# Mixing the spectral matrices inside the layer norm's stage, on three engines

## The chip, the cores and the metric

One core of a Trainium2 chip. The metric is device microseconds (us) of one execution; the kernel before takes 3382.94 us (median of 3 runs, 3381.09 to 3384.28). Abbreviations as in the profile: PE is TensorE's matrix multiplications, PEld its loads of stationary data, DVE is VectorE, ACT is ScalarE, POOL is GpSimd, SP is the engine that issues the DMAs.

## The reference, cut to what matters

The kernel computes a network of four layers on an image of 2 x 128 channels x 64 x 64. The change touches the second half of layer 2, a spectral filter over tokens that comes behind a layer norm:

```python
t = t + _L2_ffn_ref(_ln_t(t), sigma, phi, M_u, M_phi_plus, M_phi_minus, log_weights, gumbel)

y_soft  = softmax(log_weights + gumbel)                  # 4 weights
weights = one_hot(argmax(y_soft)) - y_soft + y_soft
# for each of the 4 branches i, on the first T // 2**i tokens:
out_i = stu(x_i, sigma ** 0.25, phi, M_u[i], M_phi_plus[i], M_phi_minus[i])
return sum(stacked * weights)
```

`M_phi_plus` and `M_phi_minus` are 4 x 16 matrices of 128 x 128, `M_u` is 4 x 3 of them. Since each branch is linear in its matrices, the kernel first sums the four branches' matrices with the four weights, and transforms once. The layer norm before it (`_ln_t`: over the 128 channels of each token) does not depend on these matrices, nor they on it.

## The kernel before, in words

The image lies in SBUF as X, 128 channels by 8192 tokens, in 16 chunks of 512 columns. The program is a sequence of stages. Each is one `Block` with a stream of instructions for each engine, semaphores between them, and a barrier of all engines at its end (`Stage.block`, L66 to L70); the instruction streams are written out by hand, and an engine runs its stream in order.

`spectral_bank` (L1722) runs, one after another: `mixing_weights` (L1242), `layer_norm_channels` with tag "sp" (L708), `spectral_inputs` (the transform, L1366), `spectral_slots`, `spectral_outputs`. The first two matter here.

`mixing_weights`. SP loads four small vectors, then `raw_u`, then four pieces of the large matrices (2 MB each: eight filters of plus or of minus, four branches) into two buffers, `raw[0]` and `raw[1]`; pieces 2 and 3 wait until DVE has finished with the buffer. DVE computes the four weights in a chain of operations on 128x4 (L1311 to L1332), with one Exp on ACT (L1293), and POOL raises sigma to the power 0.25 (L1281). Then, for each of four pieces, DVE sums the branches in four operations on 128x1024 (a tensor_scalar at L1339, three scalar_tensor_tensor at L1341) into `mixed[i]`, and multiplies it by sigma's power (L1354). It sums the direct matrices `Mu` the same way (128x384). POOL forms plus minus minus and plus plus minus into `both` (L1287), ACT rounds `both` to the high part `Mh` (L1298), and DVE at the end subtracts to get the low part `Ml` (L1362). PE has nothing to do in this stage.

`layer_norm_channels`. For each chunk c PE multiplies by the centring matrix (L734) into one of three PSUM banks `psC`; ACT squares it (L775) and copies it centred to its place (L776); PE sums the squares over channels (L742) into a row of `psV[b]`, one image half b for eight chunks. When eight chunks are summed, ACT takes the square root (L780, issued behind chunk 9 for b = 0 and behind chunk 15 for b = 1); DVE takes the reciprocal (L788) and splits it into a high and a low row (L790, L792); PE spreads it over the partitions (L753) into one of three banks `psR`; DVE multiplies the centred chunk by it (L805). In PE's order the spread of chunk c - 10 comes behind the variance of chunk c, and the last ten spreads come at the end; a spread waits until DVE has taken the chunk three before it. SP and POOL have nothing to do in this stage.

Of the kernel before, what the change touches and what calls it, by code (L numbers as in the profile page):

```python
# [15 lines left out]
ALU = mybir.AluOpType  # L16
ACT = mybir.ActivationFunctionType
AX = mybir.AxisListType
# [6 lines left out]
NCH = L // CH  # L25
# [16 lines left out]
NF = 16  # L42
# [665 lines left out]
def layer_norm_channels(nc, T, src, dst, tag, affine=None):  # L708
# [6 lines left out]
    with ExitStack() as ctx:  # L715
# [9 lines left out]
        S = Stage(nc, ctx, ["c_in_psum", "squared", "centred", "v_summed", "sd_done", "rstd_done", "rows_high",  # L725
                            "rows_done", "r_in_psum", "scaled", "z_done"])
        with S.block() as block:
            @block.tensor
# [40 lines left out]
            @block.scalar  # L769
            def _(e):  # L770
                for c in range(NC2):
                    e.wait_ge(S["c_in_psum"], c + 1)
                    if c >= 3:
                        e.wait_ge(S["v_summed"], c - 2)
                    e.activation(sq[c % 3][:, :], psC[c % 3][:, :], ACT.Square).then_inc(S["squared"], 1)  # L775
                    e.activation(centred(c), psC[c % 3][:, :], ACT.Copy).then_inc(S["centred"], 1)  # L776
                    if c == NCH + 1 or c == NC2 - 1:
                        b = c // NCH if c == NC2 - 1 else 0
                        e.wait_ge(S["v_summed"], (b + 1) * NCH)
                        e.activation(sd[b][:, :], psV[b][0:NT, :], ACT.Sqrt, bias=T["eps"][0:NT, 0:1]).then_inc(S["sd_done"], 1)  # L780

            @block.vector
            def _(e):
                for b in range(B):
                    e.memset(rows[b][64:128, :].bitcast(F32), 0.0)
                for b in range(B):
# [7 lines left out]
                    for c in range(b * NCH, (b + 1) * NCH):  # L794
# [9 lines left out]
                        else:  # L804
                            e.tensor_tensor(dst(c), psR[c % 3][:, :], centred(c), ALU.mult).then_inc(S["scaled"], 1)  # L805

# [431 lines left out]
UPAD = 4  # L1238
# [3 lines left out]
def mixing_weights(nc, T, G):  # L1242

    with ExitStack() as ctx:
        sb, _ = allocator(nc, ctx, "_mix")
        z, g, e1, y, oh, wt = (sb("mx_" + n, [128, 4]) for n in ("z", "g", "e", "y", "oh", "w"))  # L1250
        m1, s1, r1, free = (sb("mx_" + n, [128, 1]) for n in ("m", "s", "r", "free"))
        sig, quarter = sb("mx_sig", [128, NF]), sb("mx_quarter", [128, NF])
        raw = [sb(f"mx_raw{i}", [128, 4, NF // 2 * 128]) for i in range(2)]
        raw_u = sb("mx_rawu", [128, 4, 3 * 128])
        mixed = [sb(f"mx_mixed{i}", [128, NF // 2, 128]) for i in range(4)]
        both = [sb(f"mx_both{i}", [128, NF // 2, 128]) for i in range(4)]
        S = Stage(nc, ctx, ["small_loaded", ("mat_loaded", 4), "mu_loaded", "chain", "sig_done", "acc_step",
                            "both_done", "high_done", "split_done"])
        with S.block() as block:
            @block.sync  # L1260
            def _(e):
                row = lambda n: T[n][0, :].partition_broadcast(128)
                loads = [(z, row("log_weights")), (g, row("gumbel")), (sig, row("sigma")),
                         (quarter, T["c_quarter"])]
                for dst, src in loads:
                    e.dma_start(dst[:, :], src).then_inc(S["small_loaded"], 16)
                e.dma_start(raw_u[:, :, :], T["m_u"].rearrange("d i t e -> d i (t e)")).then_inc(S["mu_loaded"], 16)
                for part in range(2):
                    for n, name in enumerate(("m_plus", "m_minus")):
                        i = 2 * part + n  # L1270
                        if i >= 2:
                            e.wait_ge(S["acc_step"], 5 * (i - 1))
                        k0 = part * NF // 2
                        e.dma_start(raw[i % 2][:, :, :], T[name][:, :, k0:k0 + NF // 2, :].rearrange("d i k e -> d i (k e)"))\
                            .then_inc(S["mat_loaded"][i], 16)
                e.wait_ge(S["mat_loaded"][3], 16)

            @block.gpsimd
            def _(e):
                e.wait_ge(S["small_loaded"], 64)  # L1280
                e.tensor_tensor(sig[:, :], sig[:, :], quarter[:, :], ALU.pow).then_inc(S["sig_done"], 1)  # L1281
                e.memset(G["U"][:, 0, 0:UPAD], 0.0)
                e.memset(G["U"][:, 1, 0:UPAD], 0.0)
                for part in range(2):
                    e.wait_ge(S["acc_step"], 10 * (part + 1))
                    for n, op in enumerate((ALU.subtract, ALU.add)):
                        e.tensor_tensor(both[2 * part + n][:, :, :], mixed[2 * part][:, :, :], mixed[2 * part + 1][:, :, :], op)\  # L1287
                            .then_inc(S["both_done"], 1)

            @block.scalar  # L1290
            def _(e):
                e.wait_ge(S["chain"], 3)
                e.activation(e1[:, :], z[:, :], ACT.Exp).then_inc(S["chain"], 1)  # L1293
                for i in range(4):
                    e.wait_ge(S["both_done"], i + 1)
                    part, n = divmod(i, 2)
                    k0 = part * NF // 2
                    e.activation(G["Mh"][n][:, k0:k0 + NF // 2, :], both[i][:, :, :], ACT.Copy).then_inc(S["high_done"], 1)  # L1298

            @block.vector  # L1300
            def _(e):
                count = [0]

                def link(op):

                    count[0] += 1
                    op.then_inc(S["chain"], 1)
                    e.wait_ge(S["chain"], count[0])

                e.wait_ge(S["small_loaded"], 64)  # L1310
                link(e.tensor_tensor(z[:, :], z[:, :], g[:, :], ALU.add))  # L1311
                link(e.tensor_reduce(m1[:, :], z[:, :], AX.X, ALU.max))
                link(e.tensor_scalar(z[:, :], z[:, :], m1[:, 0:1], None, ALU.subtract))
                count[0] += 1
                e.wait_ge(S["chain"], 4)
                link(e.tensor_reduce(s1[:, :], e1[:, :], AX.X, ALU.add))
                link(e.reciprocal(r1[:, :], s1[:, :]))
                link(e.tensor_scalar(y[:, :], e1[:, :], r1[:, 0:1], None, ALU.mult))
                link(e.tensor_reduce(m1[:, :], y[:, :], AX.X, ALU.max))

                link(e.tensor_scalar(oh[:, :], y[:, :], m1[:, 0:1], None, ALU.is_ge))
                for i in range(1, 4):
                    link(e.tensor_reduce(s1[:, :], oh[:, 0:i], AX.X, ALU.add))
                    link(e.tensor_scalar(free[:, :], s1[:, :], -1.0, 1.0, ALU.mult, ALU.add))
                    link(e.tensor_tensor(oh[:, i:i + 1], oh[:, i:i + 1], free[:, :], ALU.mult))
                link(e.tensor_tensor(wt[:, :], oh[:, :], y[:, :], ALU.subtract))
                link(e.tensor_tensor(wt[:, :], wt[:, :], y[:, :], ALU.add))

                for c in range(NCH):
                    n = sum(c < NCH >> i for i in range(4))  # L1330
                    op = e.tensor_reduce(G["keep"][:, c:c + 1], oh[:, 0:n], AX.X, ALU.add)
                link(op)  # L1332
                steps = [0]

                def mix(dst, src):

                    for i in range(4):
                        if i == 0:
                            op = e.tensor_scalar(dst, src(i), wt[:, 0:1], None, ALU.mult)  # L1339
                        else:  # L1340
                            op = e.scalar_tensor_tensor(dst, src(i), wt[:, i:i + 1], dst, ALU.mult, ALU.add)  # L1341
                        steps[0] += 1
                        op.then_inc(S["acc_step"], 1)
                        e.wait_ge(S["acc_step"], steps[0])

                e.wait_ge(S["sig_done"], 1)
                for part in range(2):
                    k0 = part * NF // 2
                    for i in (2 * part, 2 * part + 1):
                        e.wait_ge(S["mat_loaded"][i], 16)  # L1350
                        dst = mixed[i][:, :, :]
                        mix(dst.rearrange("d k e -> d (k e)"), lambda x, i=i: raw[i % 2][:, x, :])
                        steps[0] += 1
# [1092 lines left out]
```

## Time and profile before

| | us |
|---|---|
| median of 3 runs | 3382.94 (3381.09 to 3384.28) |
| profiled execution, its own time | 3384.74 |
| its span | 3383.0 |
| PE busy, share of the span | 3071.9, 91% |
| DVE busy | 1908.1, 56% |
| ACT busy | 1419.0, 42% |
| POOL busy | 1056.3, 31% |

Times in the profile are counted from the start of the span. "Busy" is time in which an engine executes, summed; a stage may leave the busiest engine with nothing to do however high its share of the whole. The granted clock (PEclk) is the TensorE clock, 1.00 for 2.4 GHz and 0.50 for 1.2 GHz. An arrow "<-" in brackets names what ended an engine's idle time before the row.

### The profile page before, as it was taken

The page shows a single profiled execution, that of the slowest core. Times are in us where ns is not written, and L with a number is a line of the kernel's source. Part 1 is how long each engine was busy: PE and PEld are TensorE (multiplying, and loading weights), DVE is VectorE, ACT ScalarE, POOL GpSimd, SP SyncE. Part 2 cuts the span into 40 slices and gives each one's busy share as a digit, 9 for nine tenths or more (in the row PEclk, how much of TensorE's full clock was granted, in tenths as well). Part 3 has the DMA queues.
Part 4 walks back from the last instruction along what each step waited for, and adds up shares of the span by engine and source line. Part 5 has one row for each costly group of instructions (what it writes and reads, how often), then busy time and mean ns, then how long its engine had stood idle before and what let it go on. Part 6 is the DMA issues. An engine that isn't in the chain of part 4 may idle for free. (4 is left out here: it accounts for less than half of the span.)

```text
span 3383.0 us, 60840 instructions
## 1 busy us (share of the span) xinstructions
PE 3071.9 (91%) x23047; PEld 2397.8 (71%) x23047; DVE 1908.1 (56%) x3737; ACT 1419.0 (42%) x3058; POOL 1056.3 (31%) x1104
## 2 busy tenths in 40 slices
PE   5999997688873989999999999999889998999699
PEld 4777775233432568888888888888868887888555
DVE  5556585577525345555555555555336776776365
ACT  2555553111232234444444444444125666667200
POOL 3445450377521044444444444444000000000000
PEclk9999998799986999999999999999779999999799
DMA  7988850000002355454545455554200000000000
GB/s 173 186 181 181 179 152 20 13 1 1 1 3 109 140 74 76 72 79 69 79 72 82 72 76 76 73 79 69 62 6 1 1 1 1 1 1 1 8 22 28
DMA packets 407112, 213.33 MB, mean 63 GB/s; under 512 B 313972, under 2 KB 386316, under 8 KB 405036
## 3 DMA queue, kind: packets, MB, share of 16 engines
q1 hardware_dynamic: 388960, 199.27, 30.9%
q10 hardware_dynamic: 17868, 10.19, 1.4%
q8 instruction: 187, 3.06, 0.4%
q14 instruction: 97, 0.79, 0.1%
HBM read 177.82 MB, written 52.89 MB: 68 GB/s over the span
## 5 line engine op out<-in xcount | busy, mean ns | idle before, releaser
L1670 DVE TENSOR_TENSOR sl_vl_slot<-sl_psV_slot,sl_vh_slot 128x512 fp32r<-128x512 f32 x1024 | 636.1, 684 | 563.8 <-ACT sl_vh_slot L1649 563.8
L1649 ACT ACTIVATE sl_vh_slot<-sl_psV_slot 128x512 fp32r<-128x512 f32 x1024 | 529.3, 604 | 584.4 <-PE sl_psV_slot L1617 584.4
L85 PE MATMUL sl_psY_slot<-sl_vl_slot,sp_Mh_sp 128*128 128x256 f32 x2048 | 603.9, 295 | 0.0
L86 PE MATMUL sl_psY_slot<-sl_vh_slot,sp_Ml_sp 128*128 128x256 f32 x2048 | 577.8, 282 | 0.0
L87 PE MATMUL sl_psY_slot<-sl_vh_slot,sp_Mh_sp 128*128 128x256 f32 x2048 | 576.8, 282 | 0.0
L85 PEld LDWEIGHTS sl_psY_slot<-sl_vl_slot,sp_Mh_sp 128*128 128x128 f32 x2048 | 389.1, 190 | 91.0 <-issue 90.6
L86 PEld LDWEIGHTS sl_psY_slot<-sl_vh_slot,sp_Ml_sp 128*128 128x128 f32 x2048 | 390.4, 191 | 0.0
L87 PEld LDWEIGHTS sl_psY_slot<-sl_vh_slot,sp_Mh_sp 128*128 128x128 f32 x2048 | 389.8, 190 | 0.0
L1593 POOL CAST sl_fh_slot<-sl_f_slot 128x512 fp32r<-128x512 f32 x256 | 167.3, 653 | 575.5 <-PE sl_psV_slot L1617 575.5
L1595 POOL TENSOR_TENSOR sl_fl_slot<-sl_f_slot,sl_fh_slot 128x512 fp32r<-128x512 f32 x256 | 337.8, 1319 | 20.6
L2025 DVE TENSOR_TENSOR ca_ptl_ca<-ca_psT_ca,ca_pth_ca 128x512 fp32r<-128x512 f32 (+1 forms) x272 | 183.8, 676 | 170.3 <-ACT ca_pth_ca L1962 170.2
L1617 PE MATMUL sl_psV_slot<-sl_fl_slot,sl_uh_slot 64*128 64x512 f32 x1024 | 230.2, 446 | 14.5 <-POOL sl_fl_slot L1595 14.5
L1962 ACT ACTIVATE ca_pth_ca<-ca_psT_ca 128x512 fp32r<-128x512 f32 (+1 forms) x272 | 158.9, 584 | 184.9 <-PE ca_psO_ca L87 180.9
L1617 PE MATMUL sl_psV_slot<-sl_fh_slot,sl_ul_slot 64*128 64x512 f32 x1024 | 203.2, 393 | 0.0
L1617 PE MATMUL sl_psV_slot<-sl_fh_slot,sl_uh_slot 64*128 64x512 f32 x1024 | 199.9, 387 | 0.0
L696 POOL TENSOR_TENSOR na_s_na<-na_s_na,na_nmax_na 128x400 f32<-128x400 f32 x128 | 109.1, 853 | 237.0 <-DVE na_nmax_na L580 221.5
L85 PE MATMUL ca_psO_ca<-ca_ptl_ca,ca_vh_ca 128*128 128x256 f32 (+1 forms) x546 | 177.0, 324 | 0.4 <-DVE ca_ptl_ca L2025 0.4
L1888 PE MATMUL ca_psT_ca<-ident,ca_s_ca 128*128 128x128 f32 x768 | 146.0, 277 | 30.1 <-DVE ca_ptl_ca L2025 15.3
L86 PE MATMUL ca_psO_ca<-ca_pth_ca,ca_vl_ca 128*128 128x256 f32 (+1 forms) x546 | 154.6, 283 | 0.0
L87 PE MATMUL ca_psO_ca<-ca_pth_ca,ca_vh_ca 128*128 128x256 f32 (+1 forms) x546 | 154.5, 283 | 0.0
L1953 ACT ACTIVATE ca_s_ca<-ca_s_ca,ca_nm_ca 128x512 f32<-128x512 f32 (+3 forms) x216 | 144.4, 669 | 20.3 <-DVE ca_nm_ca L2014 20.3
L370 PE MATMUL na_psO_na<-na_v_na,na_pt_na 100*64 100x129 f32 x2048 | 140.9, 279 | 3.6 <-issue 3.5
(395 smaller groups left out, 6180.6 us busy)
## 6 DMA issues: line engine op xcount, KB each, us to landing
sl_f_slot<-filt_hat SPq DMA_DIRECT2D x256, 256.0 KB, 5.4
na_v_na<-na_windows SPq DMA_DIRECT2D x128, 390.0 KB
na_windows<-na_values SPq DMA_DIRECT2D x160, 113.8 KB, 6.4
na_values<-na_vo_na ACTq DMA_DIRECT2D x32, 260.0 KB, 6.7
u_hat<-fw_o_fwd SPq DMA_DIRECT2D x8, 1024.0 KB, 3.8
sl_u_slot<-u_hat SPq DMA_DIRECT2D x128, 64.0 KB, 2.2
y_hat<-sl_y_slot SPq DMA_DIRECT2D x128, 64.0 KB, 4.7
X<-in_x SPq DMA_DIRECT2D x8, 512.0 KB, 8.1
```

The lines of the kernel that those rows point to most:

```text
L85: e.matmul(out, lh, rl, start=start, stop=False)
L86: e.matmul(out, ll, rh, start=False, stop=False)
L87: return e.matmul(out, lh, rh, start=False, stop=stop)
L1593: e.tensor_copy(high, raw).then_inc(S["f_high"], 1)
L1595: e.tensor_tensor(low, raw, high, ALU.subtract).then_inc(S["f_split"], 1)
L1617: mm = e.matmul(psV[(first + par) % NPV][:, :], u_in[u % 2][pu][rows, b, :], f_in[n % NFI][pf][rows, :], start=(x == 0), stop=(x == 2))
L1649: e.activation(v_out(0, n, q), bank(4 * n + q), ACT.Copy).then_inc(S["v_high"], 1)
L1670: e.tensor_tensor(v_out(1, n, q), bank(m), v_out(0, n, q), ALU.subtract).then_inc(S["v_split"], 1)
L1888: tr = e.transpose(psT[g % 2][:, at:at + 128], row(P, t, (2 * m + j) * 128, 128), T["ident"][:, :])
L1953: e.activation(part, part, ACT.Exp, bias=nm[:, P % 2, t:t + 1], accum_out=rs[:, P % 2, t, x:x + 1])\
L1962: e.activation(pt[g % 2][0][:, 0:n], psT[g % 2][:, 0:n], ACT.Copy).then_inc(S["p_high"], 1)
L2025: e.tensor_tensor(pt[g % 2][1][:, 0:n], psT[g % 2][:, 0:n], pt[g % 2][0][:, 0:n], ALU.subtract).then_inc(S["p_low"], 1)
```

## The change

The function `mixing_weights` becomes a class `MixingWeights` whose methods are called from inside `layer_norm_channels`, so that both pieces of work are in one stage. The order on each engine in the new stage:

- SP: the four small vectors, pieces 0 and 1, pieces 2 and 3 (each behind the sum that frees its buffer), and `raw_u` last.
- ACT: the Exp of the weights; chunks 0 to 9 with the first square root; the rounding of the first two `both`; chunks 10 to 15 with the second root; the rounding of the last two.
- DVE: two memsets, the weights, the sums of pieces 0 and 1; reciprocal, rows and chunks 0 to 3; the sum of piece 2; chunks 4 to 7; the sum of piece 3; reciprocal, rows and chunks 8 to 15; the direct sum.
- POOL: the power; then for each half: two products with sigma's power (DVE's before), the two `both`; and the four low parts (DVE's before), the first two behind the first half's `both`, the last two at the end.
- PE: as before.

All buffers keep their sizes. The diff, cut (`vector_weights` holds the chain of the old function unchanged; the loads, buffers and `scalar_weights` too):

```diff
-def layer_norm_channels(nc, T, src, dst, tag, affine=None):
+def layer_norm_channels(nc, T, src, dst, tag, affine=None, beside=None):
...
+        if beside:
+            beside.begin(sb, S)
         with S.block() as block:
+            if beside:
+                @block.sync
+                def _(e):
+                    beside.sync(e)
+
+                @block.gpsimd
+                def _(e):
+                    beside.gpsimd(e)
...
             @block.scalar
             def _(e):
+                if beside:
+                    beside.scalar_weights(e)
                 for c in range(NC2):
                     e.wait_ge(S["c_in_psum"], c + 1)
...
                         e.activation(sd[b][:, :], psV[b][0:NT, :], ACT.Sqrt, bias=T["eps"][0:NT, 0:1]).then_inc(S["sd_done"], 1)
+                    if beside and c == NCH + 1:
+                        beside.scalar_high(e, 0)
+                if beside:
+                    beside.scalar_high(e, 1)
 
             @block.vector
             def _(e):
                 for b in range(B):
                     e.memset(rows[b][64:128, :].bitcast(F32), 0.0)
+                if beside:
+                    beside.vector_weights(e)
+                    beside.vector_mix(e, 0)
+                    beside.vector_mix(e, 1)
                 for b in range(B):
...
                             e.tensor_tensor(dst(c), psR[c % 3][:, :], centred(c), ALU.mult).then_inc(S["scaled"], 1)
+                        if beside and c in (3, 7):
+                            beside.vector_mix(e, 2 + c // 4)
+                if beside:
+                    beside.vector_mix_direct(e)
...
+    def sync(self, e):
...
+                if i >= 2:
+                    e.wait_ge(S["mix_done"], i - 1)
+                k0 = part * NF // 2
+                e.dma_start(self.raw[i % 2][:, :, :], T[name][:, :, k0:k0 + NF // 2, :].rearrange("d i k e -> d i (k e)"))\
+                    .then_inc(S["mat_loaded"][i], 16)
+        e.dma_start(self.raw_u[:, :, :], T["m_u"].rearrange("d i t e -> d i (t e)")).then_inc(S["mu_loaded"], 16)
+
+    def gpsimd(self, e):
...
+        for part in range(2):
+            k0 = part * NF // 2
+            for i in (2 * part, 2 * part + 1):
+                e.wait_ge(S["mix_done"], i + 1)
+                dst = self.mixed[i][:, :, :]
+                e.tensor_tensor(dst, dst, self.sig[:, k0:k0 + NF // 2].unsqueeze(2).to_broadcast([128, NF // 2, 128]), ALU.mult)\
+                    .then_inc(S["scaled_m"], 1)
+            e.wait_ge(S["scaled_m"], 2 * part + 2)
+            for n, op in enumerate((ALU.subtract, ALU.add)):
+                e.tensor_tensor(self.both[2 * part + n][:, :, :], self.mixed[2 * part][:, :, :],
+                                self.mixed[2 * part + 1][:, :, :], op).then_inc(S["both_done"], 1)
+            if part == 0:
+                self.low(e, 0)
+        self.low(e, 1)
+
+    def low(self, e, part):
+        S, G, k0 = self.S, self.G, part * NF // 2
+        for n in range(2):
+            i = 2 * part + n
+            e.wait_ge(S["high_done"], i + 1)
+            e.tensor_tensor(G["Ml"][n][:, k0:k0 + NF // 2, :], self.both[i][:, :, :], G["Mh"][n][:, k0:k0 + NF // 2, :],
+                            ALU.subtract).then_inc(S["split_done"], 1)
...
+    def scalar_high(self, e, part):
+        S, k0 = self.S, part * NF // 2
+        for n in range(2):
+            i = 2 * part + n
+            e.wait_ge(S["both_done"], i + 1)
+            e.activation(self.G["Mh"][n][:, k0:k0 + NF // 2, :], self.both[i][:, :, :], ACT.Copy).then_inc(S["high_done"], 1)
...
+    def vector_sum(self, e, dst, src, done):
+
+        S, wt = self.S, self.wt
+        for i in range(4):
+            if i == 0:
+                op = e.tensor_scalar(dst, src(i), wt[:, 0:1], None, ALU.mult)
+            else:
+                op = e.scalar_tensor_tensor(dst, src(i), wt[:, i:i + 1], dst, ALU.mult, ALU.add)
...
+    def vector_mix_direct(self, e):
+        e.wait_ge(self.S["mu_loaded"], 16)
+        self.vector_sum(e, self.G["Mu"][:, :, :].rearrange("d t e -> d (t e)"), lambda x: self.raw_u[:, x, :],
+                        self.S["mix_done"])
...
-            mixing_weights(nc, T, G)
             u_at = lambda c: flat[:, c // NCH * UL + UPAD + c % NCH * CH:c // NCH * UL + UPAD + (c % NCH + 1) * CH]
-            layer_norm_channels(nc, T, T["X"], u_at, "sp")
+            layer_norm_channels(nc, T, T["X"], u_at, "sp", beside=MixingWeights(T, G))
```

## Rows read from the trace of the kernel before

**Rows 1.** Busy us by engine (instructions) in two stretches; then clock, DMA share, GB/s:
```profile
1014.00:1066.00 52.00, 0.00 (x0) 0.00 (x1) 40.09 (x55) 5.01 (x6) 13.17 (x7) 0.50 0.47 177
1066.00:1112.00 46.00, 39.83 (x224) 30.28 (x224) 13.65 (x24) 19.10 (x35) 0.00 (x0) 0.87 0.02 6
```
**Rows 2.** PE's waits from 1066 to 1112: in total, times, longest:
```profile
PE ln_psC_sp L734 <- PEq L70: 56.5, 1, 56.5
PE ln_psR_sp L753 <- DVE ln_rows_sp L792: 2.5, 1, 2.5
```
**Rows 3.** Timeline of the mixing stage: start us, us, engine, line, operation:
```profile
1013.32 0.34 SPq L1266 DMA_DIRECT2D mx_z_mix<-in_log_weights  x1
...
1016.25 0.63 SPq L1274 DMA_DIRECT2D mx_raw_mix<-in_m_minus  x1
...
1018.94 2.93 POOL L1281 TENSOR_TENSOR mx_sig_mix<-mx_sig_mix,mx_quarter_mix 128x16 f32<-128x16 f32 x1 [6.54 <-DMA mx_quarter_mix<-in_c_quarter]
...
1019.54 0.20 ACT L1293 ACTIVATE mx_e_mix<-mx_z_mix 128x4 f32<-128x4 f32 x1 [4.97 <-DVE mx_z_mix L1313]
...
1021.35 0.16 DVE L1325 TENSOR_TENSOR mx_oh_mix<-mx_oh_mix,mx_free_mix 128x1 f32<-128x1 f32 x1
...
1023.08 0.58 DVE L1331 TENSOR_REDUCE sp_keep_sp<-mx_oh_mix 128x1 f32<-128x4 f32 x8
1026.03 0.75 DVE L1339 TENSOR_SCALAR mx_mixed_mix<-mx_raw_mix,mx_w_mix 128x1024 f32<-128x1024 f32 x1 [2.36 <-DMA mx_raw_mix<-in_m_plus]
1026.82 3.92 DVE L1341 SCALAR_TENSOR_TENSOR mx_mixed_mix<-mx_raw_mix,mx_w_mix,mx_mixed_mix 128x1024 f32<-128x1024 f32 x3
...
1036.66 1.22 DVE L1354 TENSOR_TENSOR mx_mixed_mix<-mx_mixed_mix,mx_sig_mix 128x1024 f32<-128x1024 f32 x1
...
1060.17 4.63 DVE L1362 TENSOR_TENSOR sp_Ml_sp<-mx_both_mix,sp_Mh_sp 128x1024 fp32r<-128x1024 f32 x4
```
**Rows 4.** Landing of the four large loads, in the view of their tile:
```profile
DMA to landing us min/median/max: 7.6/9.0/14.8
```
**Rows 5.** POOL's four sums (tile view, min/median/max ns), then two overlapping timeline rows:
```profile
L1287 POOL TENSOR_TENSOR mx_both_mix<-mx_mixed_mix x4: 2339/2549/2791, 1038.0 to 1056.4; 128x1024 f32<-128x1024 f32 x4
...
1040.26 2.79 POOL L1287 TENSOR_TENSOR mx_both_mix<-mx_mixed_mix 128x1024 f32<-128x1024 f32 x1
1040.89 3.25 DVE L1341 SCALAR_TENSOR_TENSOR mx_mixed_mix<-mx_raw_mix,mx_w_mix,mx_mixed_mix 128x1024 f32<-128x1024 f32 x1
```
**Rows 6.** Timeline of the layer norm's stage:
```profile
1066.03 5.18 PE L734 MATMUL ln_psC_sp<-X,centre 128*128 128x512 f32 x6 [56.47 <-PEq L70]
...
1071.04 1.05 PE L742 MATMUL ln_psV_sp<-ln_sq_sp,mean_row 128*128 128x128 f32 x8
...
1085.90 0.36 ACT L780 ACTIVATE ln_sd_sp<-ln_psV_sp,eps 32x128 f32<-32x128 f32 x1
...
1088.56 1.05 PE L742 MATMUL ln_psV_sp<-ln_sq_sp,mean_row 128*128 128x128 f32 x8
...
1096.64 0.69 DVE L805 TENSOR_TENSOR sp_U_sp<-ln_psR_sp,sp_U_sp 128x512 f32<-128x512 f32 x1 [1.51 <-PE ln_psR_sp L753]
...
1101.13 0.93 DVE L788 RECIPROCAL ln_rstd_sp<-ln_sd_sp 32x128 f32<-32x128 f32 x1
...
1108.39 0.69 DVE L805 TENSOR_TENSOR sp_U_sp<-ln_psR_sp,sp_U_sp 128x512 f32<-128x512 f32 x1 [0.16 <-PE ln_psR_sp L753]
```
**Rows 7.** Groups by form of POOL and DVE elsewhere: busy, mean ns | idle before:
```profile
L681 POOL TENSOR_TENSOR na_qm_na<-Y,na_headmask_na 128x512 f32<-128x512 f32 x63 | 65.5, 1040 | 0.0
...
L1080 DVE TENSOR_TENSOR c_m_c<-c_psB_c,c_V_c 128x512 f32<-128x512 f32 x123 | 81.7, 684 | 40.9 <-PE c_psB_c L997 40.5
...
L1103 DVE TENSOR_TENSOR c_at_c<-c_ex_c,c_ri_c 128x144 f32<-128x144 f32 x13 | 13.9, 1067 | 0.5
```
**Rows 8.** Stretches with their granted clock, columns as in the first group:
```profile
1070.00:1072.00 2.00, 2.00 (x11) 1.29 (x10) 0.00 (x0) 1.66 (x4) 0.00 (x0) 0.80 0.00 0
...
1105.00:1107.00 2.00, 2.00 (x11) 2.00 (x11) 1.84 (x4) 0.00 (x0) 0.00 (x0) 0.50 0.00 0
```

More of the change, by code:

```diff
@@ L724, in layer_norm_channels @@
         psR = [pb(f"ln_psR{i}", [128, CH]) for i in range(3)]
-        S = Stage(nc, ctx, ["c_in_psum", "squared", "centred", "v_summed", "sd_done", "rstd_done", "rows_high",
-                            "rows_done", "r_in_psum", "scaled", "z_done"])
-        with S.block() as block:
+        names = ["c_in_psum", "squared", "centred", "v_summed", "sd_done", "rstd_done", "rows_high",
+                 "rows_done", "r_in_psum", "scaled", "z_done"]
+        S = Stage(nc, ctx, names + beside.names if beside else names)
+        if beside:
+            beside.begin(sb, S)
+        with S.block() as block:
+            if beside:
[5 more added lines that the diff above has]
+                    beside.gpsimd(e)
             @block.tensor
@@ L1239 @@
 UL = L + UPAD
[L1242 to L1353, printed above, removed]
-                        e.tensor_tensor(dst, dst, sig[:, k0:k0 + NF // 2].unsqueeze(2).to_broadcast([128, NF // 2, 128]),
-                                        ALU.mult).then_inc(S["acc_step"], 1)
-                e.wait_ge(S["mu_loaded"], 16)
-                mix(G["Mu"][:, :, :].rearrange("d t e -> d (t e)"), lambda x: raw_u[:, x, :])
-                for i in range(4):
-                    part, n = divmod(i, 2)
-                    k0 = part * NF // 2
-                    e.wait_ge(S["high_done"], i + 1)
-                    e.tensor_tensor(G["Ml"][n][:, k0:k0 + NF // 2, :], both[i][:, :, :], G["Mh"][n][:, k0:k0 + NF // 2, :],
-                                    ALU.subtract).then_inc(S["split_done"], 1)
```

71 lines of the change are left out of this document (added).

## The prediction

> **What bounds the kernel now.** I read the page first: PE is busy 91% of the span, which hides that two stages before the transform run one behind the other on different engines. So I cut the stretch by stage [rows 1]. From 1014 to 1066 PE executes nothing, DVE 40.1 us and POOL 13.2 us; from 1066 to 1112 PE executes 39.8 us, DVE only 13.7 us and POOL nothing. PE's waits say the same [rows 2]: one idle time of 56.5 us, ended by the barrier at L70. The mixing stage as a whole stands on the path, and so does the layer norm behind it. The mixing stage opens at 1013.3 (first DMA issue) and its last DVE work ends at 1064.8 [rows 3]; the layer norm starts at 1066.0 and ends with the product of chunk 15 at 1109.1 [rows 6]. From 1013.3 to 1109.1 are 95.8 us, and what follows (loads of the transform, from the barrier on) is untouched. The question is therefore where the end of the joined stage comes, on the clock of this trace; 1109.1 minus that is the gain.
>
> **The joined stage, step by step.**
>
> *Start of ACT and PE.* PE's first three centrings fill the three `psC` banks and stop, since ACT now stands first at the Exp, which started at 1019.5 when DVE had the loaded vectors [rows 3]. That is unchanged, so the layer norm's ACT work begins at about 1019.8. The first root ended 15.2 us after the first variance matmul (1071.0 to 1086.3) [rows 6], so now at about 1020.4 + 15.2 = 1035.6; with PE cold at the start, as it was in its first 4 us of work (a mean clock of 0.80 from 1070 to 1072 [rows 8]), some 2 us later, at 1037.8. This turns out to be hidden by the next two steps.
>
> *Sums 0 and 1 on DVE.* The weights end at 1023.7 as before [rows 3]. Piece 0 used to end DVE's wait at 1026.0. `raw_u`, 128 x 1536 x 4 bytes = 0.75 MB, stood ahead of it and now comes last; the second large piece landed 14.8 us after its issue at 1016.3 [rows 3, 4], by when 4.75 MB had come in, so 0.75 MB are worth about 2.3 us (an estimate, between 0 and 2.3; I take 2.3). Pieces then land at 1023.7 and 1028.7. A sum is 0.75 + 3.92 us with its gaps 4.7 [rows 3]; the product with sigma's power, 1.2 us on DVE (L1354) [rows 3], leaves for POOL. Sum 0 ends at 1028.4.
>
> *POOL beside DVE.* When a POOL sum ran from 1040.3 to 1043.1, a scalar_tensor_tensor started at 1040.9 took 3.25 us, where three together take 3.92 elsewhere; it ended 1.1 us after POOL's did [rows 5, 3]. So a DVE operation on two SBUF tensors waits out a POOL operation. Sum 1 meets POOL's product of piece 0, and loses up to 2.3 us (below: 0, if DVE gets in first each time); I take 2.3: it ends at 1035.4.
>
> *ACT's hold.* POOL now owes product 1 and two `both` before ACT's two roundings end. A POOL sum of 128x1024 takes 2.34 to 2.79 us [rows 5], I take 2.45. A POOL product with a broadcast operand took 1.04 us for 512 columns [rows 7], 2.1 for 1024 (bounds 2.1 and 2.8). 1035.4 + 2.1 + 4.9 = 1042.4, and the second rounding (1.06 us) ends at 1043.5. Behind this wait on ACT stand the squares of chunks 10 to 15; PE waits for them with variance 10, and DVE for its first spread. PE stands idle for about 4.5 us. Reciprocal and rows (1.5 us) lie in this gap, even if POOL delays them.
>
> *Chunks 10 to 13 against spreads 0 to 3.* Variance 10 starts 0.6 us behind ACT, at 1044.1. Before, variance 10 started at 1088.6 and the product of chunk 3 ended at 1097.3, 8.8 us later [rows 6]. PE was idle for 2.5 us before the last spreads and its clock fell to 0.50 by 1105 [rows 2, 8]; so after this gap I charge 4.4 us of work at half the clock, 2.2 us. DVE reaches sum 2 at 1055.1.
>
> *Sums 2 and 3.* The pieces are long there. Sum 2 ends at 1059.8 (POOL's first low parts are over at about 1047.6). Meanwhile PE gets three spreads ahead and stops at the ring. Chunks 4 to 7 are 4 x 0.69 = 2.8 us: 1062.6. POOL's product 2 is over by then, so sum 3 takes 4.7: 1067.3.
>
> *Second half of the norm.* The root of b = 1 was taken long before. Reciprocal 0.93 us: 1068.3. The cast and the subtraction of the rows (0.5 us) now meet POOL's product 3 (to 1069.4) and a `both` (to 1072.1). If they wait as in [rows 5], the rows are ready at 1072.3 instead of 1068.9. The first spread takes 0.75 us, and eight DVE products paced by cold spreads 6.7 us (at mixed clocks, the same stretch from reciprocal to end was 7.95 us, of which 5.7 were these eight [rows 6]): 1079.8. These products have one input in PSUM and are not held: beside POOL the like in the convolution took 0.684 us in the mean [rows 7].
>
> *The tail.* The direct sum is new behind the norm: 384 of 1024 columns, between 0.375 x 4.7 = 1.8 us and 4.7 us; I take 2.4: 1082.2. POOL's own chain is sum 3 at 1067.3, product 3, two `both`, two low parts at 2.6, and the short DVE operations between: 1079.9. If the rows do not wait for POOL, DVE comes to the direct sum at 1076.3, waits there for the low parts instead, and ends at 1081.6: the same within 0.6 us. The low parts, 4.6 us of DVE [rows 3], are off DVE and cost POOL 10.4 us, of which only the last two are late, under the norm's end. One barrier and stage start (1064.8 to 1066.0) goes as well, already in the count.
>
> Sum: the stage ends at 1082.2 instead of 1109.1, 26.9 us earlier. Profiled execution: 3384.7 - 26.9 = 3357.8; it was 1.8 us over the median, so the median becomes 3356.0.
>
> **A rule weighed.** POOL's power took 2.93 us from 1018.9, and in it a DVE product of two SBUF tensors started at 1021.35 and took 0.16 us, unhindered [rows 3], unlike the sum at 1040.9 and unlike the 144-column product in the convolution, 1.07 us [rows 7]. The Trainium skill (SBUF — State Buffer, "Who interferes with whom") says that a DVE instruction with two SBUF inputs contends with a GpSimd instruction that reads SBUF, and that the pair of ports is held for the full instruction. By that rule the 0.16 us would have been over 0.5 us; the power shows otherwise, the sum at 1040.9 agrees. For the rows of b = 1 the one reading gives an end at 1082.2, the other 1081.6, so little hangs on it here.
>
> **Rivals.**
> - *The norm's products are held too.* If L805 waited for POOL, then about one product at b = 0 and three or four at b = 1 would lose 2.4 us each, 7 to 10 us: 3363 to 3366. For it: both engines are denser here than in the convolution. Against: 684 ns there. Chance 0.12.
> - *Better than forecast.* PE keeps its clock over the gaps (-3.3 us) and sum 1 is not held (-2.3): about 3351. The 2.5 us of idleness that cost the clock before [rows 2, 8] speaks against. 0.10.
> - *Nothing gained.* If the norm in effect stood behind all of the mixing (ACT held until all four `both`), the end would be near 1109 and the time near 3383. ACT waits only for the first two. 0.03.
> - *Slower.* POOL's product with sigma's 16 values spread by a zero stride runs on a slow path. The power took 2.93 us for 16 columns, 0.18 us each [rows 3]; at that rate a product would take 187 us and four of them 750: 4130 us. The end passes 1109 once products 1 and 3, which stand in the chain, take over 15.5 us each. Against: the product at 1.04 us for 512 columns had broadcast operands as well [rows 7]. 0.03.
>
> **How the numbers follow.** The forecast has 0.72. Its unknowns: loads no earlier (+2.3), POOL operations at 2.79 and products at 2.8 (+2), the direct sum at its upper end (+2.3), PE cold throughout the gap's work (+2), and downwards 4.5 us as in the second rival. All at once is unlikely; 3350 to 3366 takes in most of it and of the first two rivals. About 0.2% (6.8 us) is what a measurement of this kernel can tell from no change; the forecast and the first two rivals lie 17 us or more below: faster 0.94, the third gives same 0.03, the fourth slower 0.03.
>
> **What would show it.** In the changed trace: no PE idle time over 10 us in the joined stage; ACT square 0 near 6.5 us after the first DMA issue; ACT idle 4 to 6 us for `both` between chunks 9 and 10; PE waiting on the ring while DVE is in sums 2 and 3; a scalar_tensor_tensor of sum 1 at over 3 us; POOL products near 2.1 us; L805 at 0.69 us; the direct sum and POOL's last low part within 3 us of each other at the end, 69 us after the first DMA issue. It is wrong if L805 stretches to 2 to 3 us, if a POOL product takes over 5 us, or if the end comes outside 63 to 79 us.

## The result and the profile after

Median 3354.69 us (3350.16 to 3356.51, 4 runs) against 3382.02 us (3379.90 to 3384.28, 4 runs): ratio 0.9917, 95% interval 0.9900 to 0.9934, 27.3 us faster. The forecast was 26.9 us, 3356.0. The profiled execution has a span of 3354.7 us against 3383.0. In a second set of runs the same two kernels took 3348.77 and 3378.91 us, 30.1 us apart, ratio 0.9914 (0.9900 to 0.9928). How near 27.3 comes to 26.9 is therefore partly luck: the gain moved by 2.8 us from one set of runs to the other, and the second set's 3348.8 us lies just under the stated range of 3350 to 3366.

The two stages of [rows 1] are one. In the view of stretches (busy us by engine with instructions, clock, DMA share, GB/s) of the kernel after:

```profile
1015.00:1085.00 70.00, 44.21 (x224) 33.24 (x224) 44.50 (x71) 24.32 (x41) 29.27 (x15) 0.74 0.35 134
```

PE's 44.2 us and DVE's 44.5 us of work now lie beside each other, where PE's 39.8 had stood behind DVE's 40.1. POOL has 29.3 us in place of 13.2, because of the eight operations that moved to it. The 56.5 us of PE's idleness [rows 2] became four waits, listed by length (that of 3.9 us, ended by the barrier, stands before the stage's own work), in PE's waits of the kernel after from 1015.5 to 1085:

```profile
PE ln_psR_sp L765 <- DVE ln_rows_sp L814: 10.2, 1, 10.2
PE ln_psV_sp L754 <- ACT ln_sq_sp L789: 6.2, 2, 5.6
PE ln_psC_sp L746 <- PEq L70: 3.9, 1, 3.9
PE ln_psR_sp L765 <- DVE sp_U_sp L827: 3.0, 1, 3.0
```

The timeline of the joined stage, cut to the steps of the prediction; DVE, POOL and ACT stand in order of time:

```profile
1015.53 0.34 SPq L1294 DMA_DIRECT2D mx_z_sp<-in_log_weights  x1
...
1021.12 0.58 ACT L789 ACTIVATE ln_sq_sp<-ln_psC_sp 128x512 f32<-128x512 f32 x1
...
1031.44 1.42 DVE L1386 TENSOR_SCALAR mx_mixed_sp<-mx_raw_sp,mx_w_sp 128x1024 f32<-128x1024 f32 x1 [1.19 <-DMA mx_raw_sp<-in_m_minus]
...
1036.90 1.90 POOL L1317 TENSOR_TENSOR mx_mixed_sp<-mx_mixed_sp,mx_sig_sp 128x1024 f32<-128x1024 f32 x1 [4.59 <-DVE mx_mixed_sp L1388]
...
1038.88 4.69 POOL L1321 TENSOR_TENSOR mx_both_sp<-mx_mixed_sp 128x1024 f32<-128x1024 f32 x2
...
1043.60 1.06 ACT L1344 ACTIVATE sp_Mh_sp<-mx_both_sp 128x1024 fp32r<-128x1024 f32 x1 [1.29 <-POOL mx_both_sp L1321]
...
1045.20 2.08 PE L754 MATMUL ln_psV_sp<-ln_sq_sp,mean_row 128*128 128x128 f32 x8 [5.62 <-ACT ln_sq_sp L789]
...
1055.29 0.69 DVE L827 TENSOR_TENSOR sp_U_sp<-ln_psR_sp,sp_U_sp 128x512 f32<-128x512 f32 x1 [1.50 <-PE ln_psR_sp L765]
...
1063.70 3.93 DVE L1388 SCALAR_TENSOR_TENSOR mx_mixed_sp<-mx_raw_sp,mx_w_sp,mx_mixed_sp 128x1024 f32<-128x1024 f32 x3
...
1068.51 1.17 DVE L812 CAST ln_rows_sp<-ln_rstd_sp 32x128 fp32r<-32x128 f32 x1
1069.68 4.70 POOL L1321 TENSOR_TENSOR mx_both_sp<-mx_mixed_sp 128x1024 f32<-128x1024 f32 x2
1069.71 2.45 DVE L814 TENSOR_TENSOR ln_rows_sp<-ln_rstd_sp,ln_rows_sp 32x128 fp32r<-32x128 f32 x1
...
1074.35 4.68 POOL L1332 TENSOR_TENSOR sp_Ml_sp<-mx_both_sp,sp_Mh_sp 128x1024 fp32r<-128x1024 f32 x2
...
1079.34 0.69 DVE L827 TENSOR_TENSOR sp_U_sp<-ln_psR_sp,sp_U_sp 128x512 f32<-128x512 f32 x1 [0.16 <-PE ln_psR_sp L765]
...
1080.39 1.93 DVE L1388 SCALAR_TENSOR_TENSOR sp_Mu_sp<-mx_rawu_sp,mx_w_sp,sp_Mu_sp 128x384 f32<-128x384 f32 x3
```

Below, PE is called cold where its granted clock is 0.50. It was cold behind the wait for ACT and again in the last eight spreads:

```profile
1047.00:1050.00 3.00, 3.00 (x14) 2.18 (x13) 0.69 (x1) 0.97 (x3) 1.19 (x1) 0.64 0.00 0
...
1072.00:1078.00 6.00, 5.79 (x27) 5.79 (x28) 3.99 (x7) 2.12 (x2) 6.00 (x4) 0.50 0.01 3
```

From the first DMA issue to the last work are 66.8 us (1015.5 to 1082.3), where both stages took 95.8: 29.0 us less. The next stage's first matmul then came 3.2 us behind that end, where it had come 4.9 us behind; its first load landed 2.2 us sooner after its issue and the gap before the issue was 0.5 us longer. The joined stage opened 2.2 us later in this execution, through work in front of it that is the same. 29.0 + 2.2 - 0.5 - 2.2 = 28.5, against 28.3 us by the spans.

The whole kernel scatters by 3 to 11 us between executions, and the median of one and the same kernel by up to 6 us between sets of runs. Differences of one order of work to another are therefore read below from the length of the joined stage in each trace ("stage": first DMA issue to last work), with the measured time beside it. The same program gave 66.8 and 68.1 us in two traces, so a difference in stage of about 1.3 us or less says little by itself.

### The profile page after: what moved, and what is told of

It reads as the page before. It is cut to its first block and busy times, and to the rows that moved or that the text cites. A ratio compares the mean times of both kernels' runs of the same rounds, so it can differ in the third digit from the quotient of the medians.

```text
span 3354.7 us, 60816 instructions
## 1 busy us (share of the span) xinstructions
PE 3078.1 (92%) x23047; PEld 2402.8 (72%) x23047; DVE 1898.7 (57%) x3729; ACT 1419.2 (42%) x3058; POOL 1071.7 (32%) x1112
```

## The experiments

| kernel | stage, us | median, us | before, same runs | ratio (95%) |
|---|---|---|---|---|
| changed kernel | 66.8 | 3354.7 | 3382.0 | 0.9917 (0.9900 to 0.9934) |
| after_again | 68.1 | 3348.8 | 3378.9 | 0.9914 (0.9900 to 0.9928) |
| a_own_stage | 98.5 | 3381.6 | 3379.2 | 1.0007 (0.9998 to 1.0017) |
| b_dve_products_lows | 74.0 | 3355.7 | 3379.2 | 0.9932 (0.9917 to 0.9947) |
| c_high_late | 60.6 | 3345.2 | 3379.2 | 0.9894 (0.9880 to 0.9908) |
| d_rows_early | 66.5 | 3348.4 | 3379.2 | 0.9908 (0.9893 to 0.9924) |
| e_warm | 63.8 | 3341.1 | 3378.1 | 0.9887 (0.9872 to 0.9903) |
| f_rawu_first | 70.3 | 3352.3 | 3378.1 | 0.9917 (0.9903 to 0.9930) |
| g_late_and_early | 60.6 | 3345.5 | 3378.1 | 0.9899 (0.9883 to 0.9914) |
| i_sums_early | 64.1 | 3347.0 | 3378.9 | 0.9908 (0.9893 to 0.9923) |
| h_all_early | 64.2 | 3343.6 | 3378.9 | 0.9894 (0.9879 to 0.9909) |
| k_late_warm | 59.4 | 3341.9 | 3377.1 | 0.9894 (0.9876 to 0.9913) |

**The joining, or the new division of labour?**

```diff
-            layer_norm_channels(nc, T, T["X"], u_at, "sp", beside=MixingWeights(T, G))
+            mixing_alone(nc, T, G)        # the class's methods in a stage of their own
+            layer_norm_channels(nc, T, T["X"], u_at, "sp")
```

> The new division of labour (products with sigma's power and low parts on POOL) without the joining: the mixing stays in a stage of its own ahead of the layer norm. Theory 1 (the gain is the joining alone): the mixing stage, 51.5 us from first DMA issue to last work before, now ends with POOL's product, two sums and two low parts behind the last sum of DVE, and sums 2 and 3 are held by POOL's operations, so it is 52 to 56 us long and the kernel takes 3382 to 3387 us. Rival (a good part of the gain is DVE's relief, 9.5 us of products and low parts moved away): 3372 to 3376 us.

Both stages together took 98.5 us against 95.8; the mixing alone ended at 54.2 us behind its first issue, within the 52 to 56. The time was 2.4 us over the kernel before in the same runs, the interval includes no change. Its timeline shows why DVE's relief does not shorten a mixing stage by itself:

```profile
1033.07 9.80 DVE L1388 SCALAR_TENSOR_TENSOR mx_mixed_mix<-mx_raw_mix,mx_w_mix,mx_mixed_mix 128x1024 f32<-128x1024 f32 x3
...
1058.37 4.96 POOL L1332 TENSOR_TENSOR sp_Ml_sp<-mx_both_mix,sp_Mh_sp 128x1024 fp32r<-128x1024 f32 x2
```

Three operations that take 3.92 us alone take 9.80 beside POOL, and the low parts end the stage. Without the joining the new division of labour gains nothing; how much it adds inside the joined stage, the next kernel shows.

**The division of labour inside the joined stage.** The products go back to DVE behind each sum, and the four low parts behind the direct sum.

```diff
+                    beside.low(e, 0)      # on DVE, behind vector_mix_direct
+                    beside.low(e, 1)
```

> Joined stage, but the products and the low parts stay on DVE as before. Theory 1 (a chain through sums 1, 2, 3 and the tail sets the end): products 2 and 3 add 1.2 us each, the four low parts 4.6 us at the end, product 1 is 0.7 us faster: about 6 us slower than the changed kernel, 3361 us. Rival (the holding of DVE by POOL's many operations is what costs in the joined stage, so fewer of them is as good or better): 3352 to 3355 us.

The stage grew by 7.2 us (5.9 against the second trace of the changed kernel), the forecast being 6, and 4.6 of it stand at the end as foretold. So of the 29.0 us by which the stage became shorter, the joining alone, with the old division of labour, gives 21.8 (95.8 to 74.0), and the rest is DVE's relief, which pays only here. In its timeline:

```profile
1076.18 1.93 DVE L1382 SCALAR_TENSOR_TENSOR sp_Mu_sp<-mx_rawu_sp,mx_w_sp,sp_Mu_sp 128x384 f32<-128x384 f32 x3
...
1078.02 4.62 DVE L1326 TENSOR_TENSOR sp_Ml_sp<-mx_both_sp,sp_Mh_sp 128x1024 fp32r<-128x1024 f32 x4
```

The time agrees less clearly: its ratio 0.9932 is over the changed kernel's 0.9914 to 0.9917, but the intervals overlap. With the 2.9 us taken off by which the kernel before was faster in these runs, theory 1 stands at 3358 us and the rival at 3349 to 3352; the median, 3355.7, lies between. The stage speaks for theory 1 and against the rival's "as good or better"; the time leaves it open.

**ACT's hold.**

```diff
-                    if beside and c == NCH + 1:
+                    if beside and c == 13:
                         beside.scalar_high(e, 0)
```

> The first half's rounding on ACT stands behind chunk 13 instead of chunk 9. Theory 1 (ACT's hold between chunks 9 and 10, 4.1 us of wait plus 1.3 us more, is on the path): spread 0 comes when the rows are ready, at 25.9 us after the first DMA issue instead of 31.4, PE does not go cold (2.0 us), and sum 2 starts 7.5 us earlier; but POOL's low parts 0 and 1 now run beside sum 2 and hold it for up to 4 us: 3.5 to 7.5 us faster than the changed kernel, 3347 to 3351 us. Rival (the hold is hidden, since sums 2 and 3 and POOL's chain behind them fill the stage anyway): within 1 us of 3354.7.

The stage fell by 6.2 us. The product of chunk 3 ended 34.0 us behind the first issue instead of 40.5 (6.5 earlier; the forecast had 7.5), since PE stood idle for 1.1 us there in place of 5.6 and its clock stayed at 1.00:

```profile
1036.63 0.69 DVE L827 TENSOR_TENSOR sp_U_sp<-ln_psR_sp,sp_U_sp 128x512 f32<-128x512 f32 x1 [0.75 <-PE ln_psR_sp L765]
...
1039.65 4.69 POOL L1332 TENSOR_TENSOR sp_Ml_sp<-mx_both_sp,sp_Mh_sp 128x1024 fp32r<-128x1024 f32 x2 [1.55 <-ACT sp_Mh_sp L1344]
...
1043.84 1.05 DVE L1386 TENSOR_SCALAR mx_mixed_sp<-mx_raw_sp,mx_w_sp 128x1024 f32<-128x1024 f32 x1
```

(The third row is sum 2; it meets only the last 0.5 us of POOL's low parts and loses 0.3 us.) Its time, 3345.2, is below the 3347 to 3351 that were expected, which is accounted for by the runs: the kernel before was 2.9 us under its first median in them. The hold was on the path.

**The rows of the second half.**

```diff
+                        if beside and c == 7:
+                            make_rows(1)      # reciprocal, cast, subtraction
                         if beside and c in (3, 7):
                             beside.vector_mix(e, 2 + c // 4)
```

> Reciprocal and rows of the second half stand ahead of sum 3 instead of behind it, where POOL is idle. Theory 1 (POOL's chain behind sum 3 is next to the rows' hold): the rows take 1.5 us instead of 4.6 and the eight spreads lose their 1.2 us start, but sum 3 ends 1.5 us later and with it POOL's product, sums and low parts (11.3 us behind sum 3), and the direct sum waits for these: the stage ends 0.5 to 1.5 us earlier, 3353 to 3354.5 us. Rival (the rows' hold and the cold start of the spreads are wholly on the path): about 5 us faster, 3349.5 us.

The stage is 0.3 us shorter than in the shorter of the two traces of the changed kernel, and 1.6 shorter than in the other; the forecast was 0.5 to 1.5. The rows cost 1.5 us instead of 4.6, and the eight products ended 4.9 us earlier in the stage (59.6 us behind the first issue instead of 64.5), but the gain was given back by what stood behind:

```profile
1057.97 0.21 DVE L812 CAST ln_rows_sp<-ln_rstd_sp 32x128 fp32r<-32x128 f32 x1
1058.22 0.28 DVE L814 TENSOR_TENSOR ln_rows_sp<-ln_rstd_sp,ln_rows_sp 32x128 fp32r<-32x128 f32 x1
...
1069.94 5.07 POOL L1338 TENSOR_TENSOR sp_Ml_sp<-mx_both_sp,sp_Mh_sp 128x1024 fp32r<-128x1024 f32 x2
1070.23 5.85 DVE L1394 SCALAR_TENSOR_TENSOR sp_Mu_sp<-mx_rawu_sp,mx_w_sp,sp_Mu_sp 128x384 f32<-128x384 f32 x3
```

The direct sum's three operations, 1.93 us before, take 5.85, held by the two low parts. The measured time, 3348.4, is nearer to the rival's 3349.5 than to mine, but the changed kernel itself took 3348.8 in its second set, so the time does not decide. The stage does: the rival's 5 us are not in it.

**PE's clock.** PE multiplies the identity by itself 20, 10 and 38 times in its three gaps; nothing reads the result.

```diff
+                    if c == NCH + 2:
+                        if beside:
+                            e.wait_ge(S["sd_done"], 1)
+                        warm(20)
```

> PE fills its three gaps in the joined stage with 20, 10 and 38 products of the identity that nobody reads (one more wait, on the first root, for the bank). Theory 1 (cold PE costs 2.0 us in chunks 10 to 13 and 1.5 us in the last eight spreads): granted clock 1.00 from the first variance on, 3 to 3.5 us faster than the changed kernel, 3351 us. Rival (DVE and POOL pace the stage, PE's clock is of no account): 3354 to 3355 us; filling matmuls that run into the real ones would make it slower, by under 1 us.

The stage fell by 3.0 us, as expected. Stretches of it (columns as above):

```profile
1060.00:1062.00 2.00, 2.00 (x20) 2.00 (x20) 1.97 (x3) 0.00 (x0) 1.84 (x1) 1.00 0.00 0
1062.00:1064.00 2.00, 0.98 (x9) 0.79 (x8) 1.97 (x2) 0.00 (x0) 1.92 (x2) 1.00 0.00 0
1064.00:1066.00 2.00, 1.32 (x12) 1.33 (x12) 1.25 (x3) 1.06 (x1) 2.00 (x2) 1.00 0.00 0
1066.00:1068.00 2.00, 2.00 (x14) 1.75 (x13) 2.00 (x5) 1.06 (x1) 2.00 (x2) 0.85 0.03 8
1068.00:1070.00 2.00, 2.00 (x11) 2.00 (x10) 1.76 (x3) 0.00 (x0) 2.00 (x2) 0.50 0.00 0
```

The fillings of the last gap ended 1.7 us early (PE stood idle from 1063.0 to 1064.7), and the granted clock fell to 0.50 at about 1067.4, in the midst of the spreads. The kernel's median, 3341.1 us, is lower than the stage explains (9.0 us under what the changed kernel's ratio gives beside a kernel before of 3378.1, 3350.1); the other 6 us are not explained. The two traces differ by 12.7 us: 5.7 ahead of the stage, 3.0 in it and 4.1 behind it (each to the rounding). The 5.7 us are not the fillings' doing, since the second trace of the changed kernel opens its stage at 1009.0, as early as this one (1009.9), with nothing filled.

**The order of loads.**

```diff
+        e.dma_start(self.raw_u[...], T["m_u"]...)    # ahead of the four pieces, not behind
```

> The load of the direct matrices stands ahead of the large pieces, as in the kernel before. Theory 1 (sum 1 waits for piece 1, and from it hang POOL's sums, ACT's hold and all behind): pieces 0 and 1 land about 2.3 us later, 2.3 us slower than the changed kernel, 3357 us. Rival (the loads are ahead of need, or the piece's landing does not depend on the 0.75 MB): 3354.7 us.

Piece 0 was taken 12.7 us behind the first issue instead of 10.0, sum 1 ended 2.7 us later, and the stage was 3.5 us longer than in the first trace and 2.2 longer than in the second. The direction is that of theory 1. The kernel's time does not resolve it.

**Both moves.** The diffs of the two kernels above together.

> Both moves together: first rounding behind chunk 13, rows of the second half ahead of sum 3. Theory 1 (POOL's chain is the next limit): as with the first move alone or up to 1.5 us better, 3346 to 3350 us. Rival (the two moves add in full, 7.5 and 5 us): 3342 us.

The stage was 60.6 us, like that with ACT's hold removed alone: the rows' gain is again spent in the direct sum behind POOL's low parts. The rival, adding in full, is out.

**The changed kernel again**, as the measure for the two that follow.

> The changed kernel once more, on the same chip as the two below, so that they have a direct comparison. Stage from the first DMA issue to the last work 66.8 us, as in its first trace, within 0.5; ratio to the kernel before 0.990 to 0.993.

The stage was 68.1, not within 0.5 of 66.8. In the step from chunk 0 to chunk 1 DVE waited 3.28 us for PE instead of 2.15: behind the hold PE was cold for 6.3 us of work (1038.7 to about 1045.0), in the first trace for about 4 (1045.2 to about 1049.2). That step makes 1.1 of the 1.3 us. The ratio came out as expected.

**Sums moved into DVE's idle time.**

```diff
+                    if beside and b == 0:
+                        beside.vector_mix(e, 2)          # ahead of chunk 0
-                        if beside and c in (3, 7):
-                            beside.vector_mix(e, 2 + c // 4)
+                        if beside and c == 2:
+                            beside.vector_mix(e, 3)
+                        if beside and c == 4:
+                            beside.vector_mix_direct(e)
```

> Only DVE's order changes: sum 2 ahead of chunk 0 (in the 6.7 us in which DVE waits for ACT's hold to end), sum 3 behind chunk 2, the direct sum behind chunk 4; the first rounding stays behind chunk 9, rows of the second half stay behind chunk 7. Theory 1 (sum 2 is then free, sum 3 lies half beside PE's steps of 2.2 us per chunk, the direct sum too; POOL's second chain starts about 4 us earlier and still holds the rows): stage 59 to 62 us instead of 66.8, 5 to 8 us faster. Rival (POOL's low parts 0 and 1 hold sum 2 in that gap for so long that chunk 0 comes late, and the hold of the rows grows): stage 64 to 67 us.

And with ACT's first rounding behind chunk 13 and POOL's first low parts behind product 2:

> DVE's order as in the kernel with the sums early, ACT's first rounding behind chunk 13, and POOL's low parts 0 and 1 behind product 2. Theory 1 (with ACT's hold gone, sum 2 stands between the rows and chunk 0 beside PE's own work, PE does not go cold, and what is left is the norm's own length, 41 to 43 us behind a start at 5.6 us, with some holding by POOL): stage 50 to 55 us, 12 to 16 us faster than the changed kernel, 3335 to 3340 us on a chip where that one takes 3351. Rival (POOL's twelve operations, 26 us, and their waits stay the limit as they were with both earlier moves): stage 58 to 61 us.

Here my theory failed. The stages were 64.1 and 64.2 us, where I expected 59 to 62 and 50 to 55. The first lies in its rival's 64 to 67, the second above both of its ranges; its time, 3343.6 us, also misses the 3335 to 3340. The timeline of the second shows the first operation of sum 2, the three later ones of sum 3 and of the direct sum:

```profile
1036.03 2.74 DVE L1388 TENSOR_SCALAR mx_mixed_sp<-mx_raw_sp,mx_w_sp 128x1024 f32<-128x1024 f32 x1
...
1044.66 6.08 POOL L1334 TENSOR_TENSOR sp_Ml_sp<-mx_both_sp,sp_Mh_sp 128x1024 fp32r<-128x1024 f32 x2
1045.29 7.85 DVE L1390 SCALAR_TENSOR_TENSOR mx_mixed_sp<-mx_raw_sp,mx_w_sp,mx_mixed_sp 128x1024 f32<-128x1024 f32 x3
...
1055.37 7.82 DVE L1390 SCALAR_TENSOR_TENSOR sp_Mu_sp<-mx_rawu_sp,mx_w_sp,sp_Mu_sp 128x384 f32<-128x384 f32 x3
```

DVE's idle time was filled, but with operations that POOL holds, one POOL operation for each. In the view of groups by form (busy, mean ns | idle before) of this kernel and then of the one with the late rounding alone, where all these operations meet a resting POOL:

```profile
L1390 DVE SCALAR_TENSOR_TENSOR mx_mixed_sp<-mx_raw_sp,mx_w_sp,mx_mixed_sp 128x1024 f32<-128x1024 f32 x12 | 19.3, 1612 | 0.4
...
L1390 DVE SCALAR_TENSOR_TENSOR sp_Mu_sp<-mx_rawu_sp,mx_w_sp,sp_Mu_sp 128x384 f32<-128x384 f32 x3 | 7.7, 2583 | 0.1
```

```profile
L1388 DVE SCALAR_TENSOR_TENSOR mx_mixed_sp<-mx_raw_sp,mx_w_sp,mx_mixed_sp 128x1024 f32<-128x1024 f32 x12 | 15.4, 1284 | 0.4
...
L1388 DVE SCALAR_TENSOR_TENSOR sp_Mu_sp<-mx_rawu_sp,mx_w_sp,sp_Mu_sp 128x384 f32<-128x384 f32 x3 | 1.9, 618 | 0.1
```

The direct sum's three operations average 2583 ns, where they take 618 with POOL at rest, and those of the four sums 1612 ns instead of 1284. With each sum placed where POOL is busy, DVE, not PE, sets the length, and the rows and eight products come only after it. I had charged "some holding"; in this kernel it was 2.0 us for sum 2, 3.9 for sum 3 and 6.5 for the direct sum, 12.4 us in all. Without them the stage would have been 52 us long, within the 50 to 55 (an estimate from these rows). Both kernels are still 2.6 to 4.0 us of stage ahead of the changed kernel.

**The best of it.** ACT's rounding late, and PE's two remaining gaps filled (14 and 43 products).

> First rounding behind chunk 13, and PE's two remaining gaps (3.3 and 10.2 us) filled with 14 and 43 products of the identity that nobody reads. Theory 1 (the fillings of 0.24 us each now reach to the rows, so the clock stays at 1.00 and all eight last products follow each other at 0.62 to 0.70 us instead of 0.86): stage 58.5 to 59.5 us, 1.1 to 2.1 us shorter than with the first move alone. Rival (POOL's last low part and the direct sum set the end): 60.0 to 60.6 us.

```profile
1061.06 4.56 PE L765 MATMUL ln_psR_sp<-ln_rows_sp,pick_row 128*128 128x128 f32 x32 [0.57 <-DVE ln_rows_sp L826]
1061.75 4.87 DVE L839 TENSOR_TENSOR sp_U_sp<-ln_psR_sp,sp_U_sp 128x512 f32<-128x512 f32 x8 [0.75 <-PE ln_psR_sp L765]
...
1066.55 1.54 DVE L1398 TENSOR_SCALAR sp_Mu_sp<-mx_rawu_sp,mx_w_sp 128x384 f32<-128x384 f32 x1
```

The eight products took 4.9 us instead of 6.7 and began 0.5 us sooner behind the rows; 1.1 us of this was lost again where the direct sum's first operation was held by a low part (1.54 us instead of 0.41). The stage is 59.4, 1.2 us shorter than with the late rounding alone, as theory 1 had it. That is no more than two traces of one program can differ by; what carries the reading is the 1.8 us by which the eight products were faster, with the granted clock at 1.00 in all of them, where it was 0.50 with the late rounding alone. In whole-kernel time this version, the one with filled gaps alone and the one with the late rounding alone (0.9894, 0.9887, 0.9894) can't be told apart; each beats the kernel before, and their ratios lie below the changed kernel's 0.9914 to 0.9917, with intervals that still overlap.

## Why the prediction was right, step by step

Times behind the first DMA issue, forecast and measured:

| step | forecast | measured |
|---|---|---|
| ACT's first square | 6.5 | 5.6 |
| sum 1 ends | 22.1 | 21.3 |
| ACT's second rounding ends | 30.2 | 29.1 |
| product of chunk 3 ends | 41.8 | 40.5 |
| sum 2 ends | 46.5 | 45.1 |
| sum 3 ends | 54.0 | 52.1 |
| rows of the second half ready | 59.0 | 56.6 |
| last product of the norm ends | 66.5 | 64.5 |
| POOL's last low part ends | 66.6 | 63.5 |
| direct sum ends | 68.9 | 66.8 |

- *What was on the path.* That the joining is what gives the time back is shown from both sides: the new division of labour in a stage of its own gains nothing, and the joining with the old one gives 21.8 us of stage. The prediction did not divide its 26.9 us; the rest, 7.2 us of stage, is DVE's relief inside the joined stage.
- *ACT's hold* was forecast as an idle time of PE of about 4.5 us and was 5.6. Removing it gave 6.2 us, so it and the clock behind it were truly on the path. One of the prediction's signs missed here by a little: no idle time of PE was to be over 10 us, and the wait for the second rows was 10.2.
- *POOL's prices.* The product with a broadcast operand took 1.90 us (forecast 2.1), the sums 2.35 (2.45); the forecast was a little dear in both.
- *The 2.1 us at the end* are a sum of small terms, read from the table: 0.8 us up to the end of sum 1 (its hold was 0.7 us and not 2.3, against which piece 1 came 0.5 us later than forecast, and the forecast began sum 1 at 1028.4, 0.3 us ahead of its own landing of the piece), 0.5 more up to the product of chunk 3, 0.6 more up to the end of sum 3, 0.5 in the rows and 0.1 in the direct sum; the last products took back 0.4. The largest single error, 1.6 us in the hold of sum 1, was half made good by the two errors beside it, which is luck.
- *Holding by POOL.* The rows took 1.17 + 2.45 us instead of 0.5; the forecast had 3.4 us for it and it was 3.1. Sum 1 lost 0.7 us in its first operation, where I had charged 2.3, since the second piece landed when POOL's product was under way. The sign "a scalar_tensor_tensor of sum 1 at over 3 us" did not come: all took 1.28 to 1.29 us, and it was the tensor_scalar before them that was held, 1.42 us in place of 0.75. The trace agrees for the rows, 32 partitions wide, with the rule weighed from the Trainium skill (SBUF — State Buffer, "Who interferes with whom"), not with the reading by the power [rows 3]: the subtraction, with two inputs in SBUF, took 2.45 us in place of 0.28. The cast and the tensor_scalar were held as well (1.17 us in place of 0.21, 1.42 in place of 0.75); they have one input in SBUF, and the part of the rule that the prediction weighs does not speak of them.
- *The norm's products* kept 0.69 us beside POOL; the first rival is out.
- *Cold PE.* From variance 10 to the product of chunk 3 were 10.8 us, forecast 8.8 + 2.2. The filled gaps gave 3.0 us of the 3.3 that the second rival had put on it.
- *The tail.* That the rows' hold and POOL's chain would come out within 0.6 us of each other was the least obvious step; the experiment on the rows shows it, 4.9 us gained ahead of the direct sum and all but 0.3 given back in it. In the changed kernel itself the low parts ended 3.3 us before the direct sum did (the sign said within 3), so there they held nothing of it.
- *The direct sum's upper end* was wrong in the prediction, and the trace of the kernel before could have told it. The prediction bounds the sum by 4.7 us; beside two of POOL's sums it had taken 0.41 + 5.85 = 6.3 us:

```profile
1054.00 5.06 POOL L1287 TENSOR_TENSOR mx_both_mix<-mx_mixed_mix 128x1024 f32<-128x1024 f32 x2 [10.95 <-DVE mx_mixed_mix L1354]
1054.28 5.85 DVE L1341 SCALAR_TENSOR_TENSOR sp_Mu_sp<-mx_rawu_mix,mx_w_mix,sp_Mu_sp 128x384 f32<-128x384 f32 x3
```

  In the changed kernel it met no POOL operation and took 2.4 us, as forecast; with the rows early it took 6.9, with the sums early 8.9. This price, left out of the count, is also what undid the theory on the sums moved early.
- *The better rival* (about 3351) came true in part: sum 1 lost 0.7 us and not 2.3, but PE lost its clock over the gaps. *Nothing gained* is out by 29 us of stage. *The slower rival*, POOL's product on a slow path, needed over 15.5 us each; it was 1.90.

Not explained: the 2.2 us by which the transform's first load landed sooner. The second trace of the changed kernel is back near the old value (first matmul 3.7 us behind the issue; 2.0 in its first trace, 4.2 in the kernel before), so it isn't the change's doing.

## What to carry to other kernels

Two serial stages that use different engines can be worth joining even when every engine's busy share looks high; the gain is what a count of the waits in the joined order leaves, and here that count, row by row, came within 2.1 us of 29.0. In a joined order look for the one in-order engine that waits for another chain in the middle of its own (here ACT's rounding, 6.2 us) and put that wait where its operand is long ready. Filling an engine's idle time pays in full only if what it is filled with does not contend with whoever is busy then: here 12.4 us of the time filled were lost to POOL's holding.

## What the runs showed of the hardware that was not expected

- DVE and POOL take turns when both have two-input work queued: three DVE operations of 384 columns took 2.58 us each in place of 0.62 (with the sums early), one POOL operation apiece (in the kernel before, two of them already took 2.57 and 2.58), and three of 1024 columns 9.80 us in place of 3.92 (mixing in its own stage). POOL's own were stretched there too, to 3.3 us at most in place of 2.35. The 0.75 us tensor_scalar of sum 2 took 2.74 us behind one of POOL's sums.
- A gap of 1.7 us in PE's work was followed by a fall of the granted clock from 1.00 to 0.50 while PE was busy again (idle 1063.0 to 1064.7, fall at about 1067.4); with the gap filled to within 0.6 us the clock stayed at 1.00 to the end of the work.
- POOL's 128x1024 product with one operand spread by a zero stride takes 1.90 us, its sums of two full tensors 2.35.
